# Local attention in a six-stage program: another order of pairs, another start of the inverse roots

## The reference

```python
qkv = (win @ qkv_w.T + qkv_bias).reshape(-1, N, 3, NH, hd)...   # N = 64 tokens, NH = 16, hd = 8
attn = einsum('bhnm', _l2n(q), _l2n(k)) * scale                 # l2n: divided by the norm
attn = softmax(attn + rpb[None] + ATTN_MASK)
out = (attn @ v) @ proj_w.T + proj_b
x = x + _ln(out, norm1_g, norm1_b)
```

## Time and profile before

| | |
|---|---|
| three runs | 3854.44, 3876.11, 3879.24 us; median 3876.11 |
| profiled execution | 3907.29 us, its span 3905.5 us |
| mean granted TensorE clock over the span | 0.803 |
| busy over the span | PE 3235.1, PEld 2362.5, DVE 2413.6, ACT 1589.2, POOL 1141.7 us |
| local attention | first load issued at 68.01 us, last store issued by 1257.4 us |

### The profile page before, as it was taken

The page is one execution under the profiler, slowest core; times in us unless marked ns, Lnnn a source line. Parts: engine busy times, 40 slices in busy tenths (PEclk is TensorE's granted clock), DMA queues, the critical chain, the costliest instruction groups (busy, mean ns, idle before and its releaser), DMA issues. The chain is left out here.

```text
span 3905.5 us, 96986 instructions
## 1 busy us (share of the span) xinstructions
PE 3235.1 (83%) x35431; PEld 2362.5 (60%) x35431; DVE 2413.6 (62%) x6510; ACT 1589.2 (41%) x3175; POOL 1141.7 (29%) x1360
## 2 busy tenths in 40 slices
PE   2888888888886997999888888887884799988887
PEld 1565565656554775777787655665663466655555
DVE  2555555555554555888687776666664577766666
ACT  1444444444443442343300332332331577766665
POOL 0222222222222331111000155554556000035555
PEclk9656555565555998999998987777775899999999
DMA  2000000000000221000000011111111344432222
GB/s 85 15 17 16 16 17 16 17 16 17 17 16 21 68 73 39 22 21 21 6 4 4 26 44 39 43 40 37 42 33 46 94 95 98 94 84 76 78 77 72
DMA packets 298397, 162.23 MB, mean 42 GB/s; under 512 B 98300, under 2 KB 289160, under 8 KB 297736
## 3 DMA queue, kind: packets, MB, share of 16 engines
q1 hardware_dynamic: 281608, 123.16, 11.7%
q0 software_dynamic: 16384, 33.59, 2.9%
HBM read 66.74 MB, written 71.30 MB: 35 GB/s over the span
## 5 line engine op out<-in xcount | busy, mean ns | idle before, releaser
L2302 DVE TENSOR_TENSOR e_glo<-e_g,e_ghi 128x512 f16<-128x512 f32 x540 | 373.5, 692 | 250.2 <-ACT e_ghi L2209 201.1
L2204 ACT ACTIVATE e_g<-psum,b 128x512 f32<-128x512 f32 x540 | 370.3, 689 | 285.9 <-PE psum L2358 236.3
L2375 PE MATMUL psum<-w2hi,e_ghi 128*128 (+1 forms) x2160 | 399.1, 221 | 72.6 <-DVE e_glo L2302 62.8
L2188 POOL DMA_INDIRECT e_got<-ys_dram,e_idx x256 | 252.0, 984 | 609.2 <-DMA ys_dram<-e_yo 421.4
L2379 PE MATMUL psum<-w2hi,e_glo 128*128 (+1 forms) x2160 | 394.3, 220 | 6.9 <-issue 6.8
L2377 PE MATMUL psum<-w2lo,e_ghi 128*128 (+1 forms) x2160 | 393.9, 220 | 0.2
L2375 PEld LDWEIGHTS psum<-w2hi,e_ghi 128*128 128x128 f16 x2160 | 211.9, 98 | 211.4 <-issue 98.9
L592 DVE TENSOR_TENSOR pT<-pT,rpbx 128x512 f32<-128x512 f32 x128 | 90.0, 703 | 356.3 <-ACT pT L544 356.3
L1737 POOL DMA_INDIRECT xs_dram<-m_xt,m_idxl x256 | 262.9, 1027 | 114.4 <-issue 72.3
L479 POOL TENSOR_TENSOR rstd<-mv,eps 128x1 f32<-128x1 f32 x128 | 24.5, 191 | 824.8 <-DVE mv L637 824.8
L586 DVE TENSOR_REDUCE mx<-psum 128x16 f16<-128x1024 f32 x128 | 156.1, 1219 | 126.3 <-PE psum L663 126.1
(11 more groups left out here) (332 smaller groups left out, 8018.8 us busy)
## 6 DMA issues: line engine op xcount, KB each, us to landing
ys_dram<-e_yo SPq DMA_DIRECT2D x71, 256.0 KB
f_xm<-x_dram SPq DMA_DIRECT2D x32, 256.0 KB
mid_dram<-f_xm SPq DMA_DIRECT2D x32, 256.0 KB
l_t<-mid_dram SPq DMA_DIRECT2D x16, 512.0 KB
m_t<-mid_dram SPq DMA_DIRECT2D x16, 512.0 KB
res_dram<-m_rest SPq DMA_DIRECT2D x16, 512.0 KB
e_acc<-res_dram SPq DMA_DIRECT2D x32, 256.0 KB
out_dram<-e_acc SPq DMA_DIRECT2D x32, 256.0 KB
```

What stands on the lines that cost most here:

```text
L2188: gp.indirect_dma_start(out=got[:, q % 2, k, t, :], out_offset=None, in_=ys, in_offset=bass.IndirectOffsetOnAxis(idx[:, q // 2, i:i + 1], 0))\
L2204: ac.activation(g32[:, c % 4, :], bank(c % 4), ACT.Gelu, bias=bias, scale=1.0 / WSCALE)\
L2302: ve.tensor_tensor(glo[:, c % 4, :], g32[:, c % 4, :], ghi[:, c % 4, :], ALU.subtract)\
L2375: pe.matmul(o, ghi[:, c % 4, g], w2hi[:, e, f, :], start=first and t == 0, stop=False, skip_group_check=True)
```

## The change

Queries and keys are still made of the unit, but so are the value rows now: eight products of 64x64 (each half of the output channels on its own half of the partitions, with `qkv_w`'s value rows reordered on the host to match), copied by two ScalarE instructions instead of four. `xT` holds x once. The maxima are transposed into bank 7, behind the sums' columns. TensorE's list is reordered: in odd beats the products of queries, keys and values come behind the scores; projection and transposed maxima come ahead of the turned scores. x is transposed one beat earlier, in even beats. VectorE multiplies by the bias a beat later, ahead of the maxima. The scaling of layer norm and the addition go to GpSimd, as two instructions, and the store is one beat earlier. The inverse roots start as exp(-0.5 ln(n)) on ScalarE, with a table set that holds both functions loaded ahead of the stage, and one Newton step on VectorE follows. The core of the diff (waits that only follow the steps, and the removed halves of moved steps, are cut):

```diff
-            xT = sb("xT", [P, 2, 4, 2, N])
+            xT = sb("xT", [P, 2, 4, N])
+            lg = sb("lg", [P, 4 * NH])
...
-                for s in range(-5, NP * NB + 4):
+                for s in range(-6, NP * NB + 4):
...
-                    for p in range(3):
+                    for p in range(4):
                         load(Pair(0, p))
                     def beat(s):
-                        load(s + 8)
-                        q = s - 3
+                        load(s + 10)
+                        q = s - 2
...
+                            met(gp, rstd_ok, q)
+                            met(gp, xb_ok, q)
+                            met(gp, h_ok, q)
+                            gp.tensor_tensor(h1[:, q.odd, :], h1[:, q.odd, :], rstd[:, k:k + 1].to_broadcast([P, C]), ALU.mult)                                .then_inc(hr_ok.sem, 1)
+                            met(gp, hr_ok, q)
+                            gp.tensor_tensor(x1[:, q.p, :], x1[:, q.p, :], h1[:, q.odd, :], ALU.add).then_inc(x1_ok.sem, 1)
...
+                    def even(s):
+                        q = s + 2
+                        if q.real():
+                            unit(ac, tr_ps, q)
+                            met(ac, t_ps, q - 3)
+                            ac.activation(kT[:, q.u % 2].rearrange("p a t -> p (a t)"), bank(4)[:, 2 * P:4 * P], ACT.Copy)\
+                                .then_inc(kT_ok.sem, 1)
+                        turned_out(s - 2)
+                        masked(q, 0)
+                        masked(q, 1)
+                        turned_maxima(s + 1)
+                        masked(q, 2)
+                        masked(q, 3)
+                        exponential(s)
...
+                    def odd(s):
+                        turned_out(s - 2)
+                        q = s + 3
+                        if q.real():
+                            unit(ac, newton, q)
+                            unit(ac, qn_ok, q - 2)
+                            ac.activation(lg[:], nrm[:], ACT.Ln).then_inc(ln_ok.sem, 1)
+                            unit(ac, ln_ok, q)
+                            ac.activation(rsq[:, 0, :], lg[:], ACT.Exp, scale=-0.5).then_inc(seed_ok.sem, 1)
+                        turned_maxima(s + 1)
...
+                    ac.preload_act_table_set("natural_log_exp_and_others")
...
-                            done(q, ve.tensor_scalar(y0.bitcast(I32), nrm[:].bitcast(I32), -0.5, float(0x5F1FFFF9),
-                                                     ALU.mult, ALU.add), 2)
...
+                            unit(ve, seed_ok, q)
+                            done(q, ve.tensor_tensor(t, y0, y0, ALU.mult), 2)
+                            done(q, ve.scalar_tensor_tensor(out=t, in0=t, scalar=-0.5, in1=nrm[:], op0=ALU.mult, op1=ALU.mult), 3)
+                            done(q, ve.scalar_tensor_tensor(out=y0, in0=t, scalar=1.5, in1=y0, op0=ALU.add, op1=ALU.mult), 4)
...
+                            for w in range(4):
+                                for k in range(2):
+                                    i = pe.matmul(bank(5)[half(k), 256 + N * w:256 + N * w + N], xT[:, q.u % 2, w, :],
+                                                  wqkT[:, 2 * C + 64 * k:2 * C + 64 * k + 64], start=True, stop=True)
+                            i.then_inc(v_ps.sem, 1)
...
+                    def beat(s):
+                        if (s + 1).real():
+                            scores(s + 1)
+                        if s.odd:
+                            odd(s)
+                        else:
+                            even(s)
+                        project(s - 2)
+                        q = s + 1
+                        if q.real():
+                            met(pe, mx_ok, q)
+                            met(pe, mT_ok, q - 1)
+                            met(pe, on_ok, q - 3)
+                            pe.transpose(bank(7)[:, 448:512].bitcast(F16), mx2[:, q.kind(), :], ident16[:]).then_inc(mT_ps.sem, 1)
+                        if s.real():
+                            turned_scores(s)
+                        q = s - 1
+                        if q.real():
+                            sums(q)
```

More of the change, by code:

```diff
@@ L473, in beat @@
                     def beat(s):
[L474 to L482, removed]
                         q = s + 4
@@ L497, in _ @@
                 def _(ac):
[L498 to L507, removed]
                     def masked(q, g):
@@ L513, in masked, with turned_out @@
                                           bank(4)[:, 0:2 * P].rearrange("p (a w t) -> p a w t", a=2, w=2), ACT.Copy, scale=msk[:, g:g + 1]).then_inc(qm_ok.sem, 1)
[L515 to L532, removed]
+                    def turned_out(q):
                         if q.real():
@@ L536, in beat, with turned_maxima @@
                             ac.activation(onT[:, q.odd, :], bank(6)[:, 0:P], ACT.Copy).then_inc(onT_ok.sem, 1)
[L537 to L548, removed]
+                    def turned_maxima(q):
                         if q.real():
@@ L567, in _, with exponential @@
-                    beats(ac, beat)
+                            ac.activation(mT[:, q.odd, :], bank(7)[:, 448:512].bitcast(F16), ACT.Copy).then_inc(mT_ok.sem, 1)
+                    def exponential(q):
+                        if q.real():
+                            met(ac, t_ps, q)
+                            met(ac, o_ps, q - 2)
+                            for f in range(2):
+                                ac.activation(pT[:, q.odd, 2 * f:2 * f + 2].rearrange("p j w n -> p j (w n)"), turned[:, 2 * f:2 * f + 2],
+                                              ACT.Exp).then_inc(pr_ok.sem, 1)
@@ L569, in _ @@
+                    ac.preload_act_table_set("natural_log_exp_and_others")
+                    beats(ac, lambda s: odd(s) if s.odd else even(s))
                 @block.vector
                 def _(ve):
-                    C1, C2, ONE = 0.703952253, 2.38924456, 1.0 + 3.2e-7
                     def beat(s):
@@ L581, in beat @@
                                              rs[:].unsqueeze(2).to_broadcast([P, NH, HD]), ALU.mult).then_inc(on_ok.sem, 1)
+                        q = s - 1
+                        if q.real():
+                            met(ve, pr_ok, q, 2)
+                            p = pT[:, q.odd, 2:4]
+                            e = bias[:, 2:4].unsqueeze(2).to_broadcast([P, 2, 2, 2 * N])
+                            ve.tensor_tensor(p, p, e, ALU.mult).then_inc(pd_ok.sem, 1)
                         q = s + 1
@@ L699, in sums, with out_first, project, even @@
                         i.then_inc(o_ps.sem, 1)
-                    def value_rows(q):
+                    def out_first(q):
                         if q.real():
-                            unit(pe, xT_ok, q)
-                            met(pe, v_ok, q - 1)
-                            for w in range(2):
-                                i = pe.matmul(bank(5)[:, 256 + C * w:256 + C * w + C],
-                                              xT[:, q.u % 2, 2 * q.odd + w].rearrange("p r t -> p (r t)"), wqkT[:, 2 * C:3 * C],
-                                              start=True, stop=True)
-                            i.then_inc(v_ps.sem, 1)
-                    def beat(s):
-                        if (s + 1).real():
-                            scores(s + 1)
+                            met(pe, on_ok, q)
+                            met(pe, h_ok, q - 1)
+                            pe.transpose(bank(6)[:, 0:P], on[:, q.odd, :], ident[:]).then_inc(onT_ps.sem, 1)
+                    def project(q):
+                        if q.real():
+                            met(pe, onT_ok, q)
+                            pe.matmul(bank(6)[:, P:2 * P], onT[:, q.odd, :], projT[:], start=True, stop=False)
+                            pe.matmul(bank(6)[:, P:2 * P], ones16[0:64, :], pb2[:], start=False, stop=True)\
+                                .then_inc(pj_ps.sem, 1)
+                    def even(s):
                         q = s + 2
-                        if not s.odd and q.real():
+                        if q.real():
                             unit(pe, qn_ok, q)
@@ L735, in beat, with odd @@
                             i.then_inc(xT_ps.sem, 1)
[L736 removed]
+                    def odd(s):
+                        out_first(s - 2)
+                        q = s + 5
                         if q.real():
[L738 to L762 removed]
                             unit(pe, xT_ok, q)
```

128 lines of the change are left out of this document (50 added, 78 removed).

## The result

The changed kernel takes **3663.86 us** (median of 4 runs, 3638.66 to 3665.46) where the kernel before takes 3873.32 in the same comparison (4 runs): a ratio of 0.945 with a 95% interval of 0.941 to 0.950, so 209 us less. The forecast was 3695. The profiled execution after is the fastest of its four (3638.66 us, span 3636.8), the one before lay 31 us above its median, so traces are compared here stage by stage and kernels by ratios.

A forecast was written before the change was run, and what follows sets the result against it. SyncE's queue, 14.7 us for two pairs, was to bound, crossing TensorE's 11.5 to 16.1. At 14.9, (17.84 - 14.9) x 63 = 185 us gained, about 4 lost filling: profiled 3907.3 becomes 3726, median 3695; range 3650 to 3785.

The forecast's parts named there:

- The queue (14.7 us): SyncE's issuing of every load and store in local attention: 58.8 us for eight pairs, 14.7 for two, the stage's floor.
- 14.9 us a step: Local attention's time for two pairs, forecast down from 17.84 over 63 steps, 185 us gained; 14.7 to 15.2 given 0.58.
- 4 us for filling and emptying: Local attention's ends: one more beat of filling and two GpSimd steps at the end, costing about 4 us.
- Values, 0.10 a record: TensorE's value products: 16 records instead of 8, at 0.10 us each, 1.6 us in all instead of 2.30.
- The rival that wanted 0.29: TensorE's 16 value records cost 0.29 us each, 4.6 instead of 1.6: 19.1 us for two pairs, 3959; chance 0.06.
- The wait for the value copy (1.95 us): TensorE's wait before transposing the maxima, for ScalarE's value copy in bank 5: 1.95 us in two pairs, gone with bank 7.
- 0.69 us in front of the maxima: VectorE's bias product, one beat late, needs no wait for the exponentials but puts its 0.69 us before the maxima.
- Two waits that come, 0.5 us each: TensorE: even-beat projection waits for the transposed output's copy, odd-beat first transpose for VectorE's reciprocal and product; about 0.5 each.
- ScalarE, VectorE, GpSimd at nothing: Local attention's changed work on these engines, such as root, copies and scaling, was costed at no added step time.
- A clock above 0.59: Sign to look for: TensorE's granted clock in local attention rises above its present 0.59.
- The low-clock rival (15.5 to 16.1): TensorE stays at the low clock and bounds two pairs at 15.5 to 16.1 us: 3733 to 3770; chance 0.24.
- the full blocking: VectorE's two-SBUF-input operations and GpSimd's block each other fully; maxima could come 0.7 to 1.3 us late.

## Why the prediction was right, step by step

- **The queue (14.7 us) sets the forecast.** The price is exact: four cycles of eight pairs at 58.8 us, the sum made of the earlier trace rows. As a bound it is right for the mean and not for every stretch, since at 1.2 GHz throughout TensorE needs 15.4. Doubling the DMAs slows the kernel, lifting a quarter of them speeds it up, and the same edit does nothing before the change.
- **14.9 us a step.** The 0.2 us put on top for safety did not come: 14.69 in the middle. At both ends of the stage it is less, 12.1 in the first eight pairs and 12.4 in the last nine maxima (955.9 to 1005.6), when the last loads are being issued. Over the stage 0.48 us under the forecast by 63 is 30 us.
- **4 us for filling and emptying.** They did not come: the first maxima start at 90.0 instead of 92.8 us, and from the last ones to the next stage's products it is 34.2 us instead of 35.2. With the 30 us this makes the stage gain 221 us against the forecast 181. The medians are 209 apart, so some 10 us less was gained outside it, within what the runs of one kernel differ; that the time lies only 31 us under the forecast owes something to this.
- **Values, 0.10 a record.** Mis-sized: 0.066, so 1.05 us instead of 1.6, nearer to the sums' 0.057 than I chose. The rival that wanted 0.29 is out.
- **The wait for the value copy (1.95 us) goes with bank 7.** The wait went, the reason given was incomplete. Bank 7 alone makes it 18.54, with the order on TensorE and ScalarE 19.30; only the product's move on VectorE turns it into a gain, 16.66. I had costed that move as 0.69 us in front of the maxima, "where it need not wait"; it is the largest single part, 2.64 us of step when added on the kernel before, 5.7 when taken from the changed one.
- **Two waits that come, 0.5 us each.** The one for the transposed output did, 12.0 us in 600 or 0.36 each time. The one for the projection did not (0.5 us in 600), since the transposes of x stand between.
- **From 16.66 to 14.7.** The value records give 2.30 - 1.05, 1.25 us (the old ones from the earlier trace rows); the projection's wait, 1.1 us, is covered by the products placed ahead of it. That is 14.3, under the queue's 14.7. These two are read from rows, not tried apart: no run has the new order with the old value records. The sum also mixes clocks. In stretches at a granted 0.50 throughout, the 16.66 is 17.3, and less 2.35 that is 14.9, where 15.4 is measured; the 0.5 between them is not accounted for.
- **ScalarE, VectorE, GpSimd at nothing.** Shown for the root under the queue, and for the scaling with the queue lifted; with the queue lifted the root is no longer free. The one table load of the stage is at 67.25 us, ahead of the first x (1.28 us). GpSimd's long waits are for stores, not for its own work.
- **A clock above 0.59.** The column says 0.60. By the records' lengths fast stretches became more frequent: of the groups of 32 sums seen from 200 to 900 us, 25 of 92 took under 1.5 us, before 11 of 76. The low-clock rival (15.5 to 16.1) was nearly right about its own case: with the values' 0.55 us less it says 14.95 to 15.55, and 15.4 is measured where the clock stays low. It would still have been the bound. It failed because the clock did not stay low: the fast stretches pulled TensorE's mean under the queue's 14.7. The prediction made this a condition and did not price it, so that the mean came out so near the queue's figure is partly luck; at 1.2 GHz throughout, 15.4 for 14.42 would be some 60 us more, an estimate from these rows. TensorE at 92% was as near to being the bound as the queue; between them lie the 0.4 to 0.65 us that the runs with loads on ScalarE recover.

## What to carry to other kernels

Count the DMAs on an issuing queue and multiply by the price of one before making the engines faster; when what comes out is near the new step, give a share to another engine's queue. A wait that is moved by changing its buffer goes to the buffer's next neighbour unless the copy that frees it moves too, and each move shifts the wait to whatever stands in program order behind it: here three moves that are worth -0.7, -0.8 and +2.6 us one after the other. A mean step can hide two paces: look at stretches of one clock before naming the bound. Look for the instruction that waits at the head of an engine's queue and ask who stands behind it.

## What was not expected of the hardware

- A DMA costs the issuing queue 0.66 to 0.73 us whether it moves 32 rows of 128 float32 or 16.
- An operation of 64 elements a partition on VectorE, 0.20 us else, took 1.30 beside GpSimd's product and ended 0.05 us behind it, which supports the full blocking that the prediction took from the earlier trace rows:

```profile
599.18 1.26 POOL L483 TENSOR_TENSOR pT<-pT,rpbx 128x512 f32<-128x512 f32 x1
599.19 1.30 DVE L623 TENSOR_SCALAR nrm<-nrm 128x64 f32<-128x64 f32 x1
```

- With the product moved back the profile's column of the granted clock reads 1.00 from 100 to 800 us, and yet TensorE's records there are those of 1.2 GHz:

```profile
200.00:300.00 100.00, 74.58 (x1108) 51.85 (x1110) 46.53 (x100) 36.18 (x98) 31.52 (x59) 1.00 0.05 15
...
1100.00:1200.00 100.00, 76.20 (x1142) 53.42 (x1146) 45.98 (x97) 37.43 (x100) 32.55 (x60) 0.50 0.06 15
```

```profile
708.15 1.90 PE L701 MATMUL psum<-vd,pT 128*64 128x18 f32 x32
```

As many instructions and as much busy time at 1.00 as at 0.50, and sums of 1.90 us, against 1.11 in fast beats; 2 of 68 groups are fast. Where the column and the records' lengths disagree, the lengths fit the pace; whether the column lacks an entry there stays open.
- A TensorE that is busy 92 to 95% of a stretch stays mostly at 1.2 GHz here (0.58 to 0.66 in the column). The kernel with half the loads moved still has 66 of 95 groups of sums at the low level, and with the maxima's transpose moved back, where TensorE is busy only 81%, more groups are fast than in any other run, 42 of 83. What decides this was not found. The Trainium skill, "TensorE: Matmul & The Clock Gate", section "Loop structure matters more than you think", holds that back-to-back products keep the full clock; this stage does not bear that out, with 184 us of a TensorE 98% busy at a granted 0.50 (the stretch from 192 us above).
